# Two-layer recurrent block on one core: another order of ScalarE's work in layer 2

## The chip, the core and the metric

The kernel runs on one core of a Trainium2 chip. The metric is the device time of one execution in microseconds, the median of several executions.

## What is computed

The input x has 2 sequences of 1024 tokens with 256 features. Each of two layers computes `x = x + s * silu(f)`, where s is an attention of the normalised x, and f is a feed-forward part of the same normalised x. Layer 1 has attention over 1024 keys and a mixture of 64 experts. The change lies in layer 2, cut here to its core:

```python
xn = layernorm(x)
qkv = xn @ weight_qkv.T            # 16 heads of 16, 4 key/value heads
# the attention runs over the leading axis, which has length 2: token t of
# sequence 0 sees itself, token t of sequence 1 sees both
s = softmax(causal(q k / 4)) v @ weight_proj.T
h = gelu(bitlinear(xn, w_fc))      # 256 -> 1024 features
f = bitlinear(h, w_proj)           # 1024 -> 256 features
# bitlinear: layer norm of the input, then a product with ternary weights
x = x + s * silu(f)
```

## The kernel before

Layer 2 runs in eight pairs, p = 0 to 7. A pair is one tile of 128 tokens of sequence 0 with the same tile of sequence 1. Each engine has its own instruction stream, written out by hand, one loop over p each. An engine carries its stream out strictly in order, so a wait on a semaphore holds everything behind it. In this text, "round p" is the stretch from the scale `zhalf` of pair p to the scale `zhalf` of pair p+1.

What the engines do for a pair, with the function and the line in the profile:

- **TensorE** (lines 1507 to 1517): `turn_x` (1428) transposes the normalised tokens; `qkv` (1441); `fc` (1454) computes the 1024 hidden features in four groups j = 0 to 3 of eight matmuls, each group into one of three banks of PSUM, so that a group must wait until the gelu three groups before it has emptied its bank; `down1` (1487) multiplies the hidden features with the second weights in two halves, each as soon as its high and low part are there; `square_sums` (1494) ends this with the semaphore `z_ps`; `turn_att` (1464) and `project` (1472) finish the attention. Its order is `turn_x(p+1)`, `down1(p)`, `square_sums(p)`, `turn_att(p)`, `qkv(p+1)`, `project(p)`, `fc(p+1)`.
- **ScalarE** (lines 765 to 785): `gelu(p, j)` (704), four for a pair, out of PSUM; `high(p, h)` (720) rounds half h of the gelus to float16, and needs the gelus 2h and 2h+1; `square` (712) squares a half; `take_qkv` (693, 695); `gate2` (753) are two tanh of the product of `down1`, scaled by `zhalf`; `take_s1` (744) are the two copies of the attention's projection, scaled by the same `zhalf`; `half_tanh` (731) is the attention's weight.
- **VectorE** (lines 1167 to 1184): `low(p, h)` (1107) subtracts the high part from the hidden features, and needs `high(p, h)`; `moments` (1071 to 1079) of a later pair; `sum_squares` (1113, 1114, 1117); `low_x` (1096); `silu` (1064); `spreads` (1123 to 1126) and `newton` (1054 to 1059), a chain of small operations; `half_scale` (1134) writes `zhalf`; `normalise` (1086); `silu2` (1142); `score_difference` (1101). The order is `low(p, 1)`, `moments(p+2)`, `sum_squares(p)`, `low_x(p+1)`, `silu(p+3)`, `spreads(p)`, `newton`, `half_scale(p)`, `normalise(p+2)`, `silu2(p)`, `score_difference(p+1)`, `low(p+1, 0)`.
- **GpSimd** (lines 513 to 522): `attend(p)` (494, 496) needs `half_tanh(p)`; `total(p+4)` (465) for p up to 3, `add_gated(p+3)` (471, 472) for p up to 4 after `silu(p+3)`; `score_products(p+1)` (481 to 487); `finish(p)` (502, 503) needs `silu2(p)` and `take_s1(p)`.

The lines 502, 503, 494, 496, 465, 471 and 472 are tensor operations of GpSimd on data in SBUF.

Of the kernel before, what the change touches and what calls it, by code (L numbers as in the profile page):

```python
# [53 lines left out]
NP = NT // 2  # L54
# [21 lines left out]
def build(nc, q, router, Wkv, Wo, shared, sd, wgu_d, wdn_d, wqkv, wpo, wfc, wpj, out):  # L76
# [9 lines left out]
    with ExitStack() as ctx:  # L86
# [8 lines left out]
        def bk_(i):  # L95
            return two[i // 2][:, (i % 2) * 512:(i % 2) * 512 + 512]
# [193 lines left out]
        def z_bank(q):  # L290

            return bk_(5 + 2 * q)
# [232 lines left out]
        def _(sc):  # L525
# [149 lines left out]
            def gate(p):  # L675
                sc.wait_ge(acc_ready, p + 1)
                if p >= 2:
                    sc.wait_ge(x1_ready, p - 1)
                sc.activation(tg[p % 2], pair(xn, p), ACT.Tanh, scale=0.5).then_inc(gate_ready, 1)

            def high_x(p):
                sc.wait_ge(xT1_ps, p + 1)
                if p:
                    sc.wait_ge(fc_ps, 4 * p)
                sc.activation(xT_hi, bk_(0).rearrange("p (k n) -> p k n", k=KH), ACT.Copy).then_inc(xT_hi_ready, 1)

            def take_qkv(p):

                sc.wait_ge(scale_ready, p + 1)
                sc.wait_ge(qkv_ps, p + 1)  # L690
                if p >= 2:
                    sc.wait_ge(att_ready, p - 1)
                sc.activation(qkv1[p % 2], bk_(1)[:, 0:QKV1].rearrange("p (g c) -> p g c", g=NKV1), ACT.Copy,
                              scale=kvscale[p % 2][:, 1:2]).then_inc(qkv_ready, 1)
                sc.activation(kv0[p % 2], bk_(1)[:, QKV1:512].rearrange("p (g c) -> p g c", g=NKV1), ACT.Copy,
                              scale=kvscale[p % 2][:, 0:1]).then_inc(qkv_ready, 1)

            def gelu(p, j):

                n = 4 * p + j  # L700
                sc.wait_ge(fc_ps, n + 1)
                if p >= 2 and j % 2 == 0:
                    sc.wait_ge(lo_ready, 2 * (p - 2) + j // 2 + 1)
                sc.activation(hidT[p % 2][:, 512 * j:512 * j + 512], bk_(2 + n % 3), ACT.Gelu, scale=gwv[:, 0:1])\  # L704
                    .then_inc(gelu_ready, 1)

            def square(p, h):

                sc.wait_ge(gelu_ready, 4 * p + 2 * h + 2)
                if p:  # L710
                    sc.wait_ge(sqsum_ready, p)
                sc.activation(sq[:, HALF * h:HALF * h + HALF], hidT[p % 2][:, HALF * h:HALF * h + HALF], ACT.Square)\
                    .then_inc(sq_ready, 1)

            def high(p, h):

                sc.wait_ge(gelu_ready, 4 * p + 2 * h + 2)
                if p >= 2:
                    sc.wait_ge(z_ps, p - 1)
                sc.activation(hiT[p % 2][:, HALF * h:HALF * h + HALF], hidT[p % 2][:, HALF * h:HALF * h + HALF], ACT.Copy)\  # L720
                    .then_inc(hi_ready, 1)

            def own_value(p):

                if p:
                    sc.wait_ge(attT_ps, p)
                sc.activation(att_h[0], heads(kv0[p % 2][:, :, HD1:2 * HD1]), ACT.Copy).then_inc(att0_ready, 1)

            def half_tanh(p):
                sc.wait_ge(dif_ready, p + 1)  # L730
                sc.activation(td[:, :], dif[:, :], ACT.Tanh, scale=0.5 / HD1 ** 0.5).then_inc(td_ready, 1)

            def take_attT(p):
                sc.wait_ge(attT_ps, p + 1)
                sc.activation(attT, bk_(6).rearrange("p (s k n) -> p s k n", s=2, k=KH), ACT.Copy).then_inc(attT_ready, 1)

            def take_s1(p):

                sc.wait_ge(s1_ps, p + 1)
                if p >= 2:  # L740
                    sc.wait_ge(out_ready, p - 1)
                sc.wait_ge(zhalf_ready, p + 1)
                for q_ in range(GT):
                    ins = sc.activation(s1[p % 2][:, q_, :], bk_(6)[:, D * q_:D * q_ + D], ACT.Copy,
                                        scale=zhalf[p % 2][:, q_:q_ + 1])
                ins.then_inc(s1_ready, 1)

            def gate2(p):
                sc.wait_ge(zhalf_ready, p + 1)
                if p:  # L750
                    sc.wait_ge(zu_ready, GT * p)
                for q_ in range(GT):
                    sc.activation(tz[:, q_, :], z_bank(q_)[:, 0:D], ACT.Tanh, scale=zhalf[p % 2][:, q_:q_ + 1])\
                        .then_inc(ztanh_ready, 1)
# [10 lines left out]
            for p in range(NP):  # L765
                own_value(p)
                half_tanh(p)
                high(p, 1)
                for h_ in range(2):
                    square(p, h_)  # L770
                if p + 1 < NP:
                    high_x(p + 1)
                if p + 3 < NP:
                    gate(p + 3)
                take_attT(p)
                if p + 1 < NP:
                    take_qkv(p + 1)
                gate2(p)
                take_s1(p)
                if p + 1 < NP:  # L780
                    gelu(p + 1, 0)
                    gelu(p + 1, 1)
                    high(p + 1, 0)
                    gelu(p + 1, 2)
                    gelu(p + 1, 3)

# [776 lines left out]
```

## Time and profile before

| | us |
|---|---|
| median of three executions | 470.88 |
| lowest, highest | 468.42, 472.22 |
| profiled execution, its own time | 469.96 |
| its span from the first to the last instruction | 468.0 |
| granted TensorE clock, mean over the span | 0.937 of full speed |

Layer 2's pairs take from about 324 us to the end at 468 us. Over the whole span TensorE's matmuls are busy for 75%, VectorE 64%, GpSimd 57%, ScalarE 44%. These are shares over stages with different limits; what a change in a stage is worth is read from the chain of waits in that stage.

### The profile page before, as it was taken

The page shows a single profiled execution, that of the slowest core. Times are in us where ns is not written, and L with a number is a line of the kernel's source. Part 1 is how long each engine was busy: PE and PEld are TensorE (multiplying, and loading weights), DVE is VectorE, ACT ScalarE, POOL GpSimd, SP SyncE. Part 2 cuts the span into 40 slices and gives each one's busy share as a digit, 9 for nine tenths or more (in the row PEclk, how much of TensorE's full clock was granted, in tenths as well). Part 3 has the DMA queues.
Part 4 walks back from the last instruction along what each step waited for, and adds up shares of the span by engine and source line. Part 5 has one row for each costly group of instructions (what it writes and reads, how often), then busy time and mean ns, then how long its engine had stood idle before and what let it go on. Part 6 is the DMA issues. An engine that isn't in the chain of part 4 may idle for free.

```text
span 468.0 us, 6901 instructions
## 1 busy us (share of the span) xinstructions
PE 352.9 (75%) x2114; PEld 272.6 (58%) x2114; DVE 298.4 (64%) x864; ACT 204.5 (44%) x483; POOL 266.5 (57%) x272
## 2 busy tenths in 40 slices
PE   0999878687989687897998898106577767676774
PEld 0884345475877566686776777105366556565663
DVE  4929993555654253455666474246979778788766
ACT  1344242633443234643444453013563754745781
POOL 6440004177878667778888787472865566352550
PEclk9999997999999899998999999856999799799999
DMA  8760036968788798776877755490000000000000
GB/s 275 280 201 0 1 103 202 301 160 215 185 180 194 200 255 199 181 180 140 196 169 188 178 96 70 76 327 4 0 22 1 23 2 24 23 1 23 24 22 22
DMA packets 37558, 57.86 MB, mean 124 GB/s; under 512 B 6075, under 2 KB 27155, under 8 KB 37139
## 3 DMA queue, kind: packets, MB, share of 16 engines
q1 hardware_dynamic: 25235, 38.55, 25.5%
q0 software_dynamic: 12288, 18.88, 22.0%
q8 instruction: 17, 0.28, 0.3%
q14 instruction: 18, 0.15, 0.1%
HBM read 39.69 MB, written 17.73 MB: 123 GB/s over the span
## 4 chain that ended last, share of the span: by engine, by line
DVE 29%; PE 24%; DMA 13%; issue 12%; ACT 11%; POOL 10%; SPq 0%; ACTq 0%; POOLq 0%; DVEq 0%
DMA acc_d<-W,idxE 8%; POOL acc_d L457 5%; ACT W L704 3%; DMA W<-tok_d,idxE 3%; POOL W L437 3%; PE two L1320 3%; PE two L1368 3%; PE two L1284 3%; ACT A L720 2%; PE two L1193 2%; DVE F L1113 2%; DVE A L1107 2%; PE two L1380 2%; DVE ni L1054 1%; DMA x<-in_q 1%
## 5 line engine op out<-in xcount | busy, mean ns | idle before, releaser
L457 POOL DMA_INDIRECT acc_d<-W,idxE x64 | 102.4, 1599 | 30.7 <-issue 13.0
L437 POOL DMA_INDIRECT W<-tok_d,idxE x56 | 56.7, 1012 | 62.5 <-DMA tok_d<-F 45.7
L1019 DVE SCALAR_TENSOR_TENSOR W<-W,two 128x88 f32<-128x88 f32 x64 | 15.6, 244 | 63.8 <-ACT W L648 62.0
L632 ACT ACTIVATE W<-two 128x256 f32<-128x256 f32 x64 | 24.4, 381 | 51.7 <-PE two L1357 51.1
L1487 PE MATMUL two<-W,A 128*128 128x257 f16 x256 | 34.3, 294 | 16.6 <-DVE A L1107 16.6
L1487 PEld LDWEIGHTS two<-W,A 128*128 128x128 f16 x256 | 26.0, 105 | 25.0 <-issue 20.2
L1107 DVE TENSOR_TENSOR A<-W,A 128x1024 f16<-128x1024 f32 x16 | 26.7, 1670 | 21.4 <-ACT A L720 21.4
L1320 PE MATMUL two<-A,v 128*128 128x128 f32 x256 | 33.1, 284 | 6.7 <-issue 6.7
L1454 PE MATMUL two<-F,wfcT 128*128 128x256 f16 x256 | 31.0, 277 | 9.3 <-ACT W L704 9.3
L1320 PEld LDWEIGHTS two<-A,v 128*128 128x128 f32 x256 | 32.0, 199 | 8.9 <-issue 8.4
L1357 PE MATMUL two<-ident,W 128*128 128x128 f32 x112 | 22.8, 286 | 14.9 <-DMA W<-tok_d,idxE 12.7
L989 DVE TENSOR_SCALAR W<-two,W 128x256 f32<-128x256 f32 x56 | 26.8, 479 | 10.7 <-PE two L1380 6.7
L1454 PEld LDWEIGHTS two<-F,wfcT 128*128 128x128 f16 x256 | 25.0, 99 | 14.6 <-ACT W L704 10.7
L1368 PE MATMUL two<-W 128*128 128x176 f32 x160 | 31.9, 324 | 0.3 <-ACT W L639 0.2
L1357 PEld LDWEIGHTS two<-ident,W 128*128 128x128 f32 x112 | 14.2, 144 | 27.8 <-DMA W<-tok_d,idxE 17.2
L1284 PE MATMUL two<-kT,vT 128*128 128x512 f32 x64 | 30.1, 592 | 0.0
L886 DVE TENSOR_REDUCE nmax<-two 128x1 f32<-128x1024 f32 x16 | 19.6, 1223 | 14.9 <-PE two L1284 14.9
L1380 PE MATMUL two<-W 88*128 88x256 f32 x80 | 25.1, 396 | 1.1 <-DVE W L989 0.7
L1368 PEld LDWEIGHTS two<-W 128*128 128x128 f32 x160 | 25.1, 198 | 0.9 <-issue 0.9
L1428 PE MATMUL two<-ident,F 128*128 128x128 f32 x32 | 6.2, 329 | 22.9 <-DVE F L1086 22.9
L600 ACT ACTIVATE A<-two,nmax 128x1024 f32<-128x1024 f32 x16 | 17.8, 1113 | 10.0 <-DVE nmax L886 9.6
L471 POOL TENSOR_TENSOR F<-F,A 128x512 f32<-128x512 f32 x8 | 10.1, 1266 | 19.1 <-DVE F L1064 19.0
(217 smaller groups left out, 884.6 us busy)
## 6 DMA issues: line engine op xcount, KB each, us to landing
W<-in_gu SPq DMA_DIRECT2D x20, 352.0 KB
F<-in_gu SPq DMA_DIRECT2D x12, 352.0 KB
acc_d<-xn SPq DMA_DIRECT2D x8, 512.0 KB, 4.2
W<-in_dn SPq DMA_DIRECT2D x20, 176.0 KB
F<-in_dn SPq DMA_DIRECT2D x12, 176.0 KB
x<-in_q SPq DMA_DIRECT2D x4, 512.0 KB, 7.1
A<-in_Wo SPq DMA_DIRECT2D x1, 2048.0 KB, 13.0
tok_d<-xn SPq DMA_DIRECT2D x4, 512.0 KB, 4.3
```

Source lines behind the costliest of these rows:

```text
L437: pool.indirect_dma_start(out=xg[n % XR], out_offset=None, in_=tok_d[:, :], in_offset=bass.IndirectOffsetOnAxis(ap=idxE[:, n:n + 1], axis=0))\
L457: pool.indirect_dma_start(out=acc_d[n % 2][:, :], out_offset=bass.IndirectOffsetOnAxis(ap=idxE[:, n:n + 1], axis=0), in_=ysb[n % YS], in_o ...
L632: sc.activation(xgT[n % 2], bk_(2)[:, 0:D].rearrange("p (k n) -> p k n", k=KH), ACT.Copy)\
L989: ve.tensor_scalar(ysb[n % YS], bk_(3)[:, 0:D], xg[n % XR][:, D + n:D + n + 1], 0.5, ALU.mult, ALU.mult)\
L1107: ve.tensor_tensor(loT[p % 2][:, cols], hidT[p % 2][:, cols], hiT[p % 2][:, cols], ALU.subtract)\
L1284: ins = pe.matmul(two[2][:, 512 * h:512 * h + 512], vT[:, rows], kT[:, at:at + 512], start=True, stop=True)
L1320: ins = pe.matmul(bk_(1)[:, 0:P], v[:, (ORDER[t] // NP) * NP + i, :], probT[t % 2][:, i, :], start=(i == 0), stop=(i == 7))
L1357: ins = pe.transpose(bk_(2)[:, P * k:P * k + P], xg[n % XR][:, P * k:P * k + P], ident[:, :])
L1368: ins = pe.matmul(gu[n % 2], xgT[n % 2][:, k, :], wgu[r][:, n % WG, k, :], start=(k == 0), stop=(k == KH - 1))
L1380: pe.matmul(bk_(3)[:, 0:D], hT[n % 2], wdn[(n // WG) % WR][:, n % WG, :], start=True, stop=True)\
L1454: ins = pe.matmul(to, wfcT[:, k, P * c:P * c + P], part[:, k, :], start=(i == 0), stop=(i == 3))
L1487: pe.matmul(z_bank(q_)[:, 0:D + 1], part[p % 2][:, at:at + P], wpj2[:, c, 0:D + 1], start=(c == 0 and part is hiT), stop=(c == FF1 // P - ...
```

## The change

In ScalarE's loop over the pairs, `gelu(p+1, 0)` and `gelu(p+1, 1)` are put ahead of `gate2(p)`, and `high(p+1, 0)` is put between `gate2(p)` and `take_s1(p)`. Then follow `gelu(p+1, 2)` and `gelu(p+1, 3)` as before. The same instructions are issued, with the same waits, and no other engine's stream is changed. For p = 7 there is no next pair and the order stays.

```diff
@@ -775,12 +775,14 @@
                 take_attT(p)
                 if p + 1 < NP:
                     take_qkv(p + 1)
-                gate2(p)
-                take_s1(p)
                 if p + 1 < NP:
                     gelu(p + 1, 0)
                     gelu(p + 1, 1)
+                gate2(p)
+                if p + 1 < NP:
                     high(p + 1, 0)
+                take_s1(p)
+                if p + 1 < NP:
                     gelu(p + 1, 2)
                     gelu(p + 1, 3)
```

## Rows read from the trace of the kernel before

**Rows 1.** Waits, 343.7 to 468 us: us in total, times, longest us.

```profile
ACT F L753 <- DVE zhalf L1134: 18.6, 8, 3.5
```

**Rows 2.** Timeline of VectorE: start us, us, what. Five of eight `zhalf`.

```profile
343.69 0.29 DVE L1134 TENSOR_SCALAR zhalf<-ny,gwc 128x2 f32<-128x2 f32 x1
...
380.70 0.23 DVE L1134 TENSOR_SCALAR zhalf<-ny,gwc 128x2 f32<-128x2 f32 x1
...
399.18 0.23 DVE L1134 TENSOR_SCALAR zhalf<-ny,gwc 128x2 f32<-128x2 f32 x1
...
433.11 0.24 DVE L1134 TENSOR_SCALAR zhalf<-ny,gwc 128x2 f32<-128x2 f32 x1
...
447.71 0.29 DVE L1134 TENSOR_SCALAR zhalf<-ny,gwc 128x2 f32<-128x2 f32 x1
```

**Rows 3.** Chain that ended last, rounds 2 and 5: start us, us, what.

```profile
387.31 1.61 DVE A L1107
...
435.57 0.70 ACT W L704
```

**Rows 4.** Timeline of ScalarE, rounds 2 and 5; in brackets idle before, releaser.

```profile
380.96 0.84 ACT L753 ACTIVATE F<-two,zhalf 128x256 f32<-128x256 f32 x2 [3.46 <-DVE zhalf L1134]
381.69 0.84 ACT L744 ACTIVATE F<-two,zhalf 128x256 f32<-128x256 f32 x2
382.40 1.28 ACT L704 ACTIVATE W<-two,gwv 128x512 f32<-128x512 f32 x2
383.72 1.06 ACT L720 ACTIVATE A<-W 128x1024 f16<-128x1024 f32 x1
384.68 1.25 ACT L704 ACTIVATE W<-two,gwv 128x512 f32<-128x512 f32 x2
...
386.23 1.05 ACT L720 ACTIVATE A<-W 128x1024 f16<-128x1024 f32 x1
...
433.38 0.84 ACT L753 ACTIVATE F<-two,zhalf 128x256 f32<-128x256 f32 x2 [0.45 <-DVE zhalf L1134]
```

**Rows 5.** Timeline of TensorE: the matmuls of `fc` in rounds 0, 2 and 5.

```profile
342.85 2.78 PE L1454 MATMUL two<-F,wfcT 128*128 128x256 f16 x24
...
378.20 2.78 PE L1454 MATMUL two<-F,wfcT 128*128 128x256 f16 x24
...
433.62 3.66 PE L1454 MATMUL two<-F,wfcT 128*128 128x256 f16 x32
```

**Rows 6.** Timeline of GpSimd, round 2: `finish`, `attend`, `total`.

```profile
382.70 1.27 POOL L502 TENSOR_TENSOR F<-F 128x512 f32<-128x512 f32 x1 [2.46 <-ACT F L744]
...
386.42 0.62 POOL L494 TENSOR_TENSOR F<-F,td 128x256 f32<-128x256 f32 x1 [1.11 <-ACT td L731]
...
387.80 2.26 POOL L465 TENSOR_TENSOR xn<-xn,F 128x512 f32<-128x512 f32 x1
```

**Rows 7.** Timeline of VectorE, round 2: `moments`, first two sums of squares.

```profile
388.85 0.74 DVE L1071 BATCH_NORM_STATS2 st<-x 128x6 f32<-128x256 f32 x2
...
390.19 1.22 DVE L1113 TENSOR_TENSOR F<-W 128x1024 f32<-128x1024 f32 x1
391.44 0.69 DVE L1114 TENSOR_TENSOR F<-F 128x512 f32<-128x512 f32 x1
```

**Rows 8.** Timeline of VectorE ahead of `zhalf` of pair 0.

```profile
333.03 1.53 DVE L1113 TENSOR_TENSOR F<-W 128x1024 f32<-128x1024 f32 x1
334.60 1.10 DVE L1114 TENSOR_TENSOR F<-F 128x512 f32<-128x512 f32 x1
```

**Rows 9.** Timeline of GpSimd in the same stretch.

```profile
333.56 1.59 POOL L496 TENSOR_TENSOR F<-F 128x256 f32<-128x256 f32 x1
335.11 1.71 POOL L465 TENSOR_TENSOR xn<-xn,F 128x512 f32<-128x512 f32 x1
```

**Rows 10.** Busy time of TensorE and its granted clock (PEclk) in two stretches.

```profile
334.00:337.15 3.15, 0.00 (x1) 1.00 0.00 0
337.70:341.00 3.30, 3.30 (x17) 0.50 0.00 0
```

## The prediction

> **What bounds the kernel now.** I read the views in this order: the waits of layer 2, then VectorE's timeline for the length of a round, then the chain that ended last, then the timelines of the four engines beside each other. ScalarE stands at `gate2` for `zhalf` eight times, 18.6 us in all and up to 3.5 us at once [rows 1]: before that it has nothing to do, although work exists that could run. A round in the middle takes 399.18 - 380.70 = 18.48 us, the one from 433.11 to 447.71 takes 14.60 us [rows 2]. Rounds 0 to 3 have the long length and rounds 5 and 6 the short one; round 4 lies between. In round 2 the chain goes from `zhalf` through ScalarE (both tanh, both copies, all gelus, both high parts) to `low` at 387.31 on VectorE, which then works without a gap to the next `zhalf` [rows 2 to 4]. In round 5 the chain goes through TensorE's `fc` and the second gelu at 435.57 instead, and `zhalf` is there long before [rows 2, 3, 5]. So in rounds 1 to 4 what lies on ScalarE behind `zhalf` sets the pace; in rounds 5 and 6 it is what lies behind `fc`. The change moves work from the one place to the other.
>
> **Rounds 1 to 4: the gelus leave the chain.** In round 2 `fc` begins at 378.20 and its first three groups need 2.78 us, 0.93 us a group [rows 5]. In round 5, where nothing holds the second gelu but its group, it starts 435.57 - 433.62 = 1.95 us after the first matmul [rows 3, 5]. In round 2 that gives 378.20 + 1.95 = 380.15. The two gelus are spaced 1.28 - 0.70 = 0.58 us [rows 3, 4], so `gate2` could follow at 380.73, and `zhalf` releases it at 380.96 [rows 4]: both gelus are hidden in the 3.46 us of idle time, with 0.23 us to spare. From there the spacings of the same rows go on: 0.73 us for `gate2` (high part at 381.69), 0.96 us for the high part (384.68 - 383.72; copies at 382.65), 0.71 us for the copies (gelu 2 at 383.36), 1.55 us from gelu 2 to the second high part (386.23 - 384.68), which starts at 384.91 rather than 386.23. **Gain: 1.32 us in each of four rounds**, at this point of the chain. `fc`'s fourth group, which waited for the first gelu, comes some 2 us earlier as well; it was not late.
>
> What comes earlier on ScalarE meets GpSimd, though, and this takes some of it back. `finish` waits for the copies, which end at 383.46 now rather than at 382.53, 0.93 us later, while `half_tanh` and the low parts are earlier. The trace shows what happens when the two engines meet. Line 502 takes 1.27 us, and `total` has the same shape; in round 2 it starts at 387.80, lasts 2.26 us and so ends 1.14 us after `low`, which ran until 388.92 [rows 3, 6]. And ahead of pair 0's `zhalf` the two take turns: line 496 lasts 1.59 us (started just behind line 1113), line 1114 lasts 1.10 us rather than 0.69 us, `total` 1.71 us [rows 7 to 9]. One engine's operation is held until the other's ends, and a held one goes next. (The Trainium skill, page SBUF — State Buffer, section Who interferes with whom, says that a VectorE operation with two inputs in SBUF and a GpSimd operation that reads SBUF block each other for the whole instruction. By that rule the operations with one input in SBUF, as `moments`, are free; the trace agrees, since line 1071 takes 0.74 us for its two operations beside `total` and none of them is held [rows 7].)
>
> In the order after the change: the first `low` now runs from 382.8 to 384.0, ahead of `finish`, whose two operations of 1.27 us follow until about 386.55. The second `low` is ready at 386.03 and held to 386.55, ending at 387.65. That is as long (1.6 us) as before, when `attend` held it: no gain, no loss. Then come line 494 (0.62 us) and line 496 (the 0.7 us up to `total`'s start [rows 6]) until 389.0, in the time of `moments`, which `total` used before. Line 1113 (390.19 before [rows 7]) wants to start at 388.9, and is held by 0.1 us. `total` is next in the queue when line 1113 ends, and line 1114 is held for its length, 1.14 us. So where `total` exists (rounds 0, 1 and 2, as it is called for p up to 3 and the round behind `zhalf` of p has the `attend` of p+1) the gain is nearly gone. Rounds 1 and 2: -1.32 + 0.1 + 1.14 = **-0.1 us each**. Rounds 3 and 4 have no `total`: -1.32 + 0.1 = **-1.2 us each**. The bounds of this cost are 0 (GpSimd gets through in other gaps) and 1.5 us (the holds of both `low` and the two sums fully on top).
>
> **Round 0: neither.** Here `fc` begins at 342.85, only 0.84 us ahead of `zhalf` at 343.69, where in round 2 the lead is 2.50 us [rows 2, 5]. The second gelu starts at 342.85 + 1.95 = 344.80, and `gate2` behind it at 345.38, not at 344.01. It loses 1.37 us and wins back the same 1.32 us; the second high part stays where it is, within 0.1 us. But `finish` is now later by more than 2 us and the hold on the sums comes here too: 0.05 + 0.1 + 1.14 = **+1.25 us**.
>
> **Rounds 5 and 6: the change costs.** `gate2` started at 433.38 [rows 4], when `fc` had just begun (433.62). It and the copies filled the time until the second group was there at 435.57. Now they stand behind the second gelu: 0.73 + 0.73 us come on the chain, less 0.14 us because a tanh can follow a gelu 0.58 us after its start while the high part had to wait 0.72 us for its end. That is **+1.32 us** until the second high part, and here this chain ends in the squares and sums. The GpSimd side: the copies end 3.7 us later (438.68 rather than 433.38 + 0.73 + 0.84 = 434.95), `finish` ends at about 441.6, and `attend` (0.62 + 0.73 us), which used to be done beside `low`, now falls on lines 1113 and 1114. Line 494 holds the one by 0.2 us; line 496 costs the other about 0.4 us, as in rows 8 (1.10 - 0.69 us). Sum **+1.9 us each** (bounds 1.3 and 2.3).
>
> **Pair 7** has the same order as before: nothing.
>
> The sum: +1.25 - 0.1 - 0.1 - 1.2 - 1.2 + 1.9 + 1.9 = **+2.4 us**. Against the profiled execution's own 469.96 us that is 472.4 us. The median of the runs shown is 0.9 us above that execution, so 470.88 + 2.4 = 473.3 us. The bounds: with GpSimd's cost at nothing everywhere, 0.05 - 4 x 1.32 + 2 x 1.32 = -2.6 us; with all of its upper ends, about +4 us.
>
> **Rivals.**
> - *The holds by GpSimd don't add up* (gain of the reordering alone): -2.6 us, 468.3 us. For it: in round 2 the same two engines collide already and the cost there is hardly on the chain, and the order of few tenths of a microsecond decides. Against it: rows 8 and 9 show the very pattern. Chance 0.22.
> - *TensorE's clock falls at the wrong place* (slower). Ahead of pair 0's `zhalf` TensorE idles for 3.15 us and then works at 0.50 (1.2 GHz) from 337.70 to 341.00 [rows 10]; this is in `turn_att`, `qkv` and `project`, and it is why `fc`'s lead there is 1.66 us shorter. After the change the idle time of TensorE in a round is shifted: the gap inside `fc` goes, and the gap ahead of `square_sums` grows by some 1.2 us in rounds 1 and 2, since the second half of `down1` runs 1.3 us earlier while the sums come only 0.1 us earlier. If the clock falls there, the second gelu starts at 381.81, `gate2` behind it at 382.39 rather than at 380.96, and the round loses 1.43 us against my sum. It decides only in the new order: before, 2.50 us of lead covered it. Two or three such rounds give +5.3 to +6.7 us, 476.2 to 477.6 us. For it: round 0. Against it: rounds 1 and 3 of the kernel before have stretches at 0.50 too, but during `down1`, where they cost nothing. Chance 0.17. (The Trainium skill, page TensorE: Matmul & The Clock Gate, section What's actually happening, has the array at half rate after idleness and at full rate after sustained work. Before pair 0 the trace agrees.)
> - *It does nothing*: gains and losses cancel, or the second gelu is just too late to be covered in all rounds: 470.9 us, chance 0.11.
>
> My forecast has 0.5.
>
> **How the numbers follow.** No change can be told from a change below 1% (4.7 us) here. Faster by more than that needs 466.2 us, beyond even the first rival: 0.04. Slower by more than that needs 475.6 us: the clock rival nearly whole, and a little of the forecast's upper end: 0.19. The rest, 0.77, is within 1%. The range takes in most of the first rival and of the clock rival: 468.6 to 476.8 us.
>
> **What the profile after would show.** In round 2: two gelus ahead of `gate2`, no idle time between `fc`'s third and fourth group, `gate2` within 0.1 us of `zhalf`'s end, line 720's second start 4.0 us after `gate2` rather than 5.3 us. Round 3 near 17.3 us. Line 1114 near 1.8 us in rounds 0 to 2, and `total` near 2.3 us. Rounds 5 and 6 near 16.5 us, with ScalarE waiting for `fc` and no longer for `zhalf`. The prediction is wrong if `total` finds its place inside `moments` (rounds 1 and 2 then gain over a microsecond), if rounds 5 and 6 don't lengthen, or if a stretch of clock 0.50 lies on `qkv` or `project` in rounds 1 to 4.

## The result, and the profile after

The changed kernel takes 475.88 us (median of 20 executions, 470.32 to 478.72) against 471.35 us (20 executions of the kernel before). The ratio is **1.0073, 95% interval 1.0041 to 1.0105: +3.4 us**. It leaves out executions over 1.5% above the fastest of their kernel (of the changed one four, with the profiled one of 478.72 us), and so is less than the 4.5 us between the medians. The forecast was +2.4 us and "within 1%".

The profiled execution has a span of 476.7 us, 8.7 us more than before, and 4.2 us of these lie ahead of `zhalf` of pair 0, in work that the change doesn't touch. So the rounds are compared, not the spans. In its profile the lines of VectorE and TensorE are two higher: `zhalf` is line 1136, `low` 1109, the sums 1115, 1116 and 1119, `fc` 1456. The timeline of VectorE, `zhalf` of pairs 0, 2, 3, 5 and 6, answers to [rows 2]:

```profile
347.88 0.23 DVE L1136 TENSOR_SCALAR zhalf<-ny,gwc 128x2 f32<-128x2 f32 x1
...
387.15 0.23 DVE L1136 TENSOR_SCALAR zhalf<-ny,gwc 128x2 f32<-128x2 f32 x1
...
405.30 0.23 DVE L1136 TENSOR_SCALAR zhalf<-ny,gwc 128x2 f32<-128x2 f32 x1
...
438.32 0.24 DVE L1136 TENSOR_SCALAR zhalf<-ny,gwc 128x2 f32<-128x2 f32 x1
...
454.65 0.29 DVE L1136 TENSOR_SCALAR zhalf<-ny,gwc 128x2 f32<-128x2 f32 x1
```

All eight of them, in both profiles, give the length of each round in us:

| round | before | after | measured | forecast |
|---|---|---|---|---|
| 0 | 18.54 | 19.70 | +1.16 | +1.25 |
| 1 | 18.47 | 19.57 | +1.10 | -0.1 |
| 2 | 18.48 | 18.15 | -0.33 | -0.1 |
| 3 | 18.47 | 18.77 | +0.30 | -1.2 |
| 4 | 15.46 | 14.25 | -1.21 | -1.2 |
| 5 | 14.60 | 16.33 | +1.73 | +1.9 |
| 6 | 14.65 | 16.36 | +1.71 | +1.9 |
| all | 118.67 | 123.13 | +4.46 | +2.4 |

Rounds 0, 2, 4, 5 and 6 came as forecast. Rounds 1 and 3 are 1.2 and 1.5 us above it. ScalarE's timeline shows round 2 as it was meant, and then round 5 (it answers to [rows 4]):

```profile
385.73 0.69 ACT L704 ACTIVATE W<-two,gwv 128x512 f32<-128x512 f32 x1 [1.77 <-PE two L1456]
386.60 0.69 ACT L704 ACTIVATE W<-two,gwv 128x512 f32<-128x512 f32 x1 [0.19 <-PE two L1456]
387.42 0.84 ACT L753 ACTIVATE F<-two,zhalf 128x256 f32<-128x256 f32 x2
388.14 1.05 ACT L720 ACTIVATE A<-W 128x1024 f16<-128x1024 f32 x1
389.09 0.84 ACT L744 ACTIVATE F<-two,zhalf 128x256 f32<-128x256 f32 x2
...
391.35 1.09 ACT L720 ACTIVATE A<-W 128x1024 f16<-128x1024 f32 x1
...
439.91 0.69 ACT L704 ACTIVATE W<-two,gwv 128x512 f32<-128x512 f32 x1 [1.77 <-PE two L1456]
440.78 0.69 ACT L704 ACTIVATE W<-two,gwv 128x512 f32<-128x512 f32 x1 [0.19 <-PE two L1456]
441.37 0.83 ACT L753 ACTIVATE F<-two,zhalf 128x256 f32<-128x256 f32 x2
```

In round 2 both gelus run in the time in which ScalarE stood idle, and the tanh starts 0.27 us after `zhalf` begins (0.26 us before). The second high part starts 3.93 us after the tanh rather than 5.27 us: 1.34 us won. In round 5 `zhalf` begins at 438.32, and the tanh, which could follow it, stands behind the second gelu until 441.37.

What takes the gain back in round 2 is seen on GpSimd and VectorE. Their two timelines, cut to this place (they answer to [rows 6, 7]):

```profile
394.57 0.73 POOL L496 TENSOR_TENSOR F<-F 128x256 f32<-128x256 f32 x1
395.25 1.27 POOL L465 TENSOR_TENSOR xn<-xn,F 128x512 f32<-128x512 f32 x1
```

```profile
395.43 2.17 DVE L1115 TENSOR_TENSOR F<-W 128x1024 f32<-128x1024 f32 x1
397.64 0.69 DVE L1116 TENSOR_TENSOR F<-F 128x512 f32<-128x512 f32 x1
...
449.57 1.10 DVE L1116 TENSOR_TENSOR F<-F 128x512 f32<-128x512 f32 x1
```

`total` (line 465) starts 0.18 us ahead of the first sum, and this lasts 2.17 us instead of 1.22 us. In round 5 it is `attend` that holds the second sum, 1.10 us instead of 0.69 us.

The rest of the loss is TensorE's clock. The busy time of TensorE with its granted clock (the number behind the busy time and its count) in four stretches: the first two lie ahead of `zhalf` of pair 1, the third ahead of that of pair 2, the last ahead of that of pair 3:

```profile
358.30:360.90 2.60, 0.00 (x0) 1.00 0.00 0
362.10:366.00 3.90, 3.90 (x17) 0.56 0.00 0
381.70:384.60 2.90, 2.90 (x21) 1.00 0.02 6
...
399.90:403.40 3.50, 3.50 (x16) 0.53 0.02 5
```

From 362 to 366 us and from 400 to 403 us `qkv` and `project` run mostly at half clock (1.2 GHz); from 381.7 to 384.6 they run at full clock (2.4 GHz). The first gelu ahead of the gate of pair 1 starts at 367.75, after `zhalf` at 367.58, where for pair 2 it is 1.4 us ahead of it. So rounds 1 and 3, which begin with these two, are the long ones. The first stretch is the idle time ahead of the sums' product. Such long rounds are no oddity of this execution: the experiments below have one in a profile of 469.26 us and one in a profile of 470.74 us.

### The profile page after: what moved, and what is told of

Same layout as the page of the kernel before. It is cut to its first block, busy times and chain, and to the rows that moved or that the text cites. A ratio compares the mean times of both kernels' runs of the same rounds, so it can differ in the third digit from the quotient of the medians.

```text
span 476.7 us, 6901 instructions
## 1 busy us (share of the span) xinstructions
PE 357.1 (75%) x2114; PEld 276.9 (58%) x2114; DVE 298.9 (63%) x864; ACT 204.9 (43%) x483; POOL 274.1 (58%) x272
## 4 chain that ended last, share of the span: by engine, by line
PE 36%; DVE 22%; DMA 12%; ACT 11%; issue 10%; POOL 8%; SPq 0%; ACTq 0%; POOLq 0%; DVEq 0%
DMA acc_d<-W,idxE 6%; DMA W<-tok_d,idxE 4%; PE two L1286 4%; PE two L1370 3%; ACT A L720 3%; POOL acc_d L457 3%; PE two L1230 3%; DVE F L1115 3%; PE two L1322 3%; PE two L1443 3%; PE two L1195 3%; PE two L1382 2%; POOL W L437 2%; PE two L1456 2%; PE two L1474 2%
## 5 line engine op out<-in xcount | busy, mean ns | idle before, releaser
L457 POOL DMA_INDIRECT acc_d<-W,idxE x64 | 102.8, 1606 | 33.0 <-issue 14.7
L1489 PE MATMUL two<-W,A 128*128 128x257 f16 x256 | 32.1, 280 | 24.6 <-DVE A L1109 24.6
L1489 PEld LDWEIGHTS two<-W,A 128*128 128x128 f16 x256 | 24.4, 99 | 31.9 <-issue 28.6
L1109 DVE TENSOR_TENSOR A<-W,A 128x1024 f16<-128x1024 f32 x16 | 23.0, 1438 | 16.6 <-ACT A L720 16.6
L1286 PE MATMUL two<-kT,vT 128*128 128x512 f32 x64 | 32.1, 625 | 0.0
L888 DVE TENSOR_REDUCE nmax<-two 128x1 f32<-128x1024 f32 x16 | 19.6, 1224 | 18.4 <-PE two L1286 18.4
L1456 PE MATMUL two<-F,wfcT 128*128 128x256 f16 x256 | 29.6, 275 | 0.0
L704 ACT ACTIVATE W<-two,gwv 128x512 f32<-128x512 f32 x32 | 21.2, 697 | 16.1 <-PE two L1456 16.1
L502 POOL TENSOR_TENSOR F<-F 128x512 f32<-128x512 f32 x7 | 10.4, 1488 | 26.2 <-ACT F L744 26.2
```

Of the source, the lines that this page charges most:

```text
L457: pool.indirect_dma_start(out=acc_d[n % 2][:, :], out_offset=bass.IndirectOffsetOnAxis(ap=idxE[:, n:n + 1], axis=0), in_=ysb[n % YS], in_o ...
L1109: ve.tensor_tensor(loT[p % 2][:, cols], hidT[p % 2][:, cols], hiT[p % 2][:, cols], ALU.subtract)\
L1286: ins = pe.matmul(two[2][:, 512 * h:512 * h + 512], vT[:, rows], kT[:, at:at + 512], start=True, stop=True)
L1456: ins = pe.matmul(to, wfcT[:, k, P * c:P * c + P], part[:, k, :], start=(i == 0), stop=(i == 3))
L1489: pe.matmul(z_bank(q_)[:, 0:D + 1], part[p % 2][:, at:at + P], wpj2[:, c, 0:D + 1], start=(c == 0 and part is hiT), stop=(c == FF1 // P - ...
```

## The experiments

Each ratio is against the kernel before, timed beside it; an interval reaches 0.3 to 0.6% (1.3 to 2.8 us) to either side. The diffs are shortened: they show the order of the calls, and leave out conditions that stay and, at `...`, other lines. All but two are against the changed kernel; the high part alone and the control of `total` are against the kernel before. "Rounds" are the lengths from the profile of that kernel, in us, before: 18.5, 18.5, 18.5, 18.5, 15.5, 14.6, 14.7.

**The new order in rounds 5 and 6 alone**, that of before in the others. The condition `ahead` stands in both places of the change; where it is false, the two gelus and the high part follow the copies.

```diff
-                if p + 1 < NP:
+                ahead = 5 <= p < LAST
+                if ahead:
```

> The new order only in rounds 5 and 6, where fc begins after zhalf; rounds 0 to 4 keep the order of before. My theory (in these rounds gate, copies and high part line up behind the second gelu): rounds 5 and 6 about 16.3 us instead of 14.6 us, +3.5 us in all, ratio 1.007, and rounds 0 to 4 unchanged. Rival (the loss of the changed kernel comes from TensorE's clock and from GpSimd in the rounds before): no change, ratio 1.000.

Measured: ratio 1.0062 (1.0030 to 1.0093), +2.9 us. Rounds 18.5, 18.5, 18.4, 18.5, 15.5, **16.33, 16.36**. The last two are those of the changed kernel, and the others those of before: the loss at the end of the layer is the order's own, and it is most of the result.

This profile also shows what a half clock on `qkv` and `project` costs in the old order, ahead of `zhalf` of pair 3 at 401.35 (TensorE's busy time and clock, then ScalarE):

```profile
395.60:399.00 3.40, 3.40 (x18) 0.52 0.02 5
```

```profile
401.61 0.84 ACT L753 ACTIVATE F<-two,zhalf 128x256 f32<-128x256 f32 x2 [2.01 <-DVE zhalf L1141]
```

The tanh still waits for `zhalf` and starts 0.26 us behind it, and round 3 has its 18.48 us. So in the old order this costs nothing; in the new one it costs 1.4 us (below).

**The new order in rounds 1 to 4 alone.**

```diff
-                if p + 1 < NP:
+                ahead = 1 <= p <= 4
+                if ahead:
```

> The new order only in rounds 1 to 4. My theory: rounds 1 and 2 18.1 us, rounds 3 and 4 17.3 and 14.2 us, so -3.1 us where TensorE's clock is full during qkv and project; each round whose gate finds the clock at 0.50 there is 1.4 us longer. With one or two such rounds -1.7 to -0.3 us, ratio 0.996 to 0.999. Rival (the clock does not matter): -3.1 us, ratio 0.993. Rival (what the middle rounds gain is always taken back): 1.000 or more.

Measured: 0.9934 (0.9902 to 0.9965), -3.1 us. Rounds 18.50, **18.23, 18.12, 18.80, 14.26**, 14.60, 14.65. Together with the run before this takes the change apart: what it gains in the middle it gives back at the end. Round 0 is in neither run; with its +1.2 us the parts make +1.0 us by the ratios, against +3.4 us, and the 2.4 us between are within the intervals of the three ratios taken together. In the profiles the parts are +3.3, -1.5 and +1.2 us against +4.5 us: the changed kernel's has one more round at half clock (1.4 us). Round 3 was the long one here too, with TensorE's clock at 0.50 from 394.2 to 397.6 us, ahead of `zhalf` of pair 3. By the ratio my rival that the clock does not matter came closer (0.993), though the interval takes in both; the profile has one such round, and the median of the timed executions is 1 us below the profiled one, so this run alone doesn't decide between them.

**The gelus ahead, the copies ahead of the high part.**

```diff
                 gate2(p)
-                high(p + 1, 0)
                 take_s1(p)
+                high(p + 1, 0)
```

> Two gelus ahead of the gate in all rounds, but the copies again ahead of the high part, so that finish is released 1 us earlier. The second high part starts at the same time as in the changed kernel. If only ScalarE's order counts, the time is that of the changed kernel, +3.4 us against before. If GpSimd's collisions with the sums cost what the trace shows (0.94 us each in rounds 0 to 2), finish comes earlier and total fits beside moments again: rounds 0 to 2 about 0.9 us shorter each, +0.6 us against before.

Measured: 0.9995 (0.9968 to 1.0022), 3.6 us better than the changed kernel's ratio. But not for the reason that I gave. Rounds 19.33, 19.44, 17.92, 16.97, 13.94, 16.41, 16.45. The first sum is held as before (2.18 us), since `total` is still late. What is gone is the hold of the second `low` (VectorE's timeline, round 2):

```profile
385.01 1.53 DVE L1108 TENSOR_TENSOR A<-W,A 128x1024 f16<-128x1024 f32 x1 [0.68 <-ACT A L720]
387.52 1.23 DVE L1108 TENSOR_TENSOR A<-W,A 128x1024 f16<-128x1024 f32 x1 [0.98 <-ACT A L720]
```

`finish` now collides with the first `low`, which has time, and the second lasts 1.23 us rather than 1.54 us. That is 0.1 to 0.3 us a round in rounds 1, 2 and 4 against the changed kernel. This profile also has one round of half clock less than that of the changed kernel (1.4 us). The rounds of the two profiles differ by 2.7 us; what is left of the 3.6 us isn't explained.

**The high part alone ahead of the copies**, the gelus behind the gate as before.

```diff
                 gate2(p)
-                take_s1(p)
                 gelu(p + 1, 0); gelu(p + 1, 1); high(p + 1, 0)
+                take_s1(p)
```

> Only the third part of the change: the gelus stay behind the gate, but the first high part goes ahead of the copies. On ScalarE alone nothing changes for the second high part, so if only ScalarE's order counts: ratio 1.000. If GpSimd's collisions count: finish is released 2.3 us later and total falls on line 1113 in rounds 0 to 2, 0.9 to 1.1 us each, and up to 0.4 us in the others: +3 to +4 us, ratio 1.006 to 1.009.

Measured: **1.0213 (1.0153 to 1.0273), +10 us**, far more than I expected. Rounds 19.53, 18.90, 20.73, 20.22, 15.62, 15.74, 15.79. Round 1, whose gate finds the clock full, is 0.43 us longer than before, rounds 5 and 6 are 1.1 us longer: there the copies (0.72 us) are on the chain, plus 0.4 us of hold. I had expected 0.9 to 1.1 us in the first and at most 0.4 us in the last two, so the places are wrong, if not the sum. In rounds 2 and 3 TensorE's clock is at half for 6.8 us, over the whole of `qkv` and `project` (busy time and clock of TensorE):

```profile
377.50:384.30 6.80, 6.80 (x26) 0.50 0.01 2
398.00:404.80 6.80, 6.64 (x26) 0.50 0.01 2
```

and `fc` begins at 384.79, 1.45 us behind `zhalf` (383.34), where it led by 2.50 us in [rows 2, 5]. ScalarE waits for `fc` behind the gate, and the high part and the copies follow only then. The rounds of this profile give +7.9 us, and 0.7 us more lie ahead of round 0; the last 1.4 us aren't assigned.

**The hold of the sums taken away by moving `total`.** First to before the attention of pair 0:

```diff
+            for i in range(3, NP):
+                total(i)
             score_products(0)
             add_gated(2)
-            total(3)
             for p in range(NP):
                 attend(p)
-                if p + 4 < NP:
-                    total(p + 4)
```

> The changed kernel, with the totals of pairs 4 to 7 done early by GpSimd, in its idle time before the attention of pair 0, so that none falls on the sums. If the hold of line 1113 by total is a cost on the chain: rounds 0 to 2 0.9 us shorter each, so 2.8 us faster than the changed kernel, +0.6 us against before, and the sums take 1.23, 0.69, 0.42 us. If it is hidden: the time of the changed kernel, +3.4 us.

Measured: 1.0033 (1.0000 to 1.0067). Rounds **17.28, 17.27, 17.36, 17.27, 14.25**, 16.33, 16.37: without a hold by `total`, and with the clock at full speed throughout, rounds 0 to 3 are 1.2 us shorter than before each, which is the whole gain of the order. But `zhalf` of pair 0 comes 41.1 us after pair 0's gate (ScalarE's first tanh of the layer) rather than 37.0 us. GpSimd's and VectorE's timelines show why:

```profile
315.31 6.13 POOL L465 TENSOR_TENSOR xn<-xn,F 128x512 f32<-128x512 f32 x5
```

```profile
314.26 1.10 DVE L1063 TENSOR_TENSOR nt<-ny 128x4 f32<-128x4 f32 x1
315.40 1.19 DVE L1064 SCALAR_TENSOR_TENSOR nt<-nt,nv 128x4 f32<-128x4 f32 x1
316.62 1.18 DVE L1065 SCALAR_TENSOR_TENSOR ny<-nt,ny 128x4 f32<-128x4 f32 x1
...
321.49 0.16 DVE L1063 TENSOR_TENSOR nt<-ny 128x4 f32<-128x4 f32 x1
```

The roots of pair 0 are operations of 4 elements in a row, 0.16 us each. Six of them wait for one whole operation of GpSimd each, five for a `total`: 1.1 to 1.2 us. An engine's idle time was not free, because the other engine's chain ran beside it.

**`total` behind `zhalf`**, in three kernels: with the new order for p up to 4, with the order of before (the control), and with the changed kernel's order in all rounds.

```diff
                 attend(p)
-                if p + 4 < NP:
-                    total(p + 4)
 ...
+                if p + 4 < NP:
+                    pool.wait_ge(zhalf_ready, p + 1)
+                    total(p + 4)
                 if p < LAST:
                     finish(p)
```

> The new order only for p up to 4, and total(p+4) of GpSimd moved from behind attend(p) to behind zhalf of pair p, where GpSimd idles, so that it meets neither the sums nor the chain ahead of zhalf. If hold and clock are what ate the gain: rounds 0 to 3 17.3 us, round 4 14.3 us, rounds 5 and 6 14.6 us as before, so -6 us in all, ratio 0.987. If the place of total doesn't matter, it is the run with the order in rounds 1 to 4 over again, ratio 0.993. If total now holds normalise and with it the first low part to the chain's cost, 0.995 or more.

> The kernel before with total(p+4) moved behind zhalf of pair p and ScalarE's order untouched: the control. My theory: total ran in the time of moments there and cost nothing, so moving it changes little: rounds 18.4 to 18.5 us, ratio 0.998 to 1.000 (line 1117 of pair 0 is freed of its hold of 1.1 us, but that is before round 0). Rival (total is a cost in either order): 2 us faster, 0.996.

> The changed kernel in all rounds, with total(p+4) behind zhalf of pair p. My theory: rounds 0 to 3 17.3 us where the clock is full, round 4 14.3 us, rounds 5 and 6 16.3 us as in the changed kernel: -2.5 us against before, ratio 0.994 to 0.995. The distance to the run with the new order for p up to 4 alone is then what rounds 5 and 6 cost, 3.4 us. Rival (the place of total doesn't matter): ratio 1.007.

| kernel | ratio | 95% | rounds |
|---|---|---|---|
| new order for p up to 4 | 0.9915 | 0.9879 to 0.9951 | 17.89, 17.89, 17.94, 17.88, 14.24, 14.61, 14.64 |
| order of before | 0.9976 | 0.9942 to 1.0009 | 18.38, 18.41, 18.38, 18.37, 15.46, 14.59, 14.66 |
| order as changed | 0.9973 | 0.9936 to 1.0010 | 17.89, 17.88, 17.95, 17.57, 14.25, 16.32, 16.38 |

The control says that `total` was no cost in the old order (0.1 us a round). With the new order the rounds are shorter than before, but 17.9 us and not 17.3: the third expectation of the first came in part. `total` is followed by `finish`, which now takes its turn ahead of the first `low` (both timelines, round 1 of the first kernel):

```profile
363.76 1.26 POOL L502 TENSOR_TENSOR F<-F 128x512 f32<-128x512 f32 x1 [1.26 <-ACT F L745]
365.10 2.13 POOL L503 TENSOR_TENSOR x<-x,F 128x512 f32<-128x512 f32 x1
```

```profile
360.98 1.68 DVE L1094 TENSOR_SCALAR F<-x,mv,ny 128x256 f32<-128x256 f32 x2
...
363.84 4.48 DVE L1115 TENSOR_TENSOR A<-W,A 128x1024 f16<-128x1024 f32 x2
```

The two `low` together last 4.48 us; unheld, one takes 1.23 us. `normalise` (line 1094) is held first, so `low` is late and `finish` is ahead of it. The difference between the first and the third kernel is in rounds 5 and 6, 3.4 us there, as expected; the ratios differ by 0.6% (2.7 us).

**All totals early, but behind pair 0's transposes**, new order for p up to 4.

```diff
+            pool.wait_ge(xT_hi_ready, 1)
+            for i in range(3, NP):
+                total(i)
             score_products(0)
 ...
```

> The new order for p up to 4 and all totals of GpSimd in its idle time before pair 0's attention, but only once pair 0's transposes have been taken, so that they no longer hold the roots of pair 0. If the early totals of the run before cost its 4 us only by holding these roots: zhalf of pair 0 no later than before, rounds 0 to 3 17.3 us, round 4 14.3 us, rounds 5 and 6 14.6 us, -6 us in all, ratio 0.987. If pair 1's roots or the products of pair 0 are held to the chain's cost instead: 0.990 to 0.994. If totals anywhere before the rounds cost what they save: 0.995 or more.

Measured: 0.9911 (0.9878 to 0.9945). Rounds 18.04, 17.29, 17.27, 17.29, 14.24, 14.62, 14.64, -5.3 us in all; `zhalf` of pair 0 comes 38.1 us after its gate (37.0 before), so -4.2 us, which is the ratio. The roots of pair 1 are held now, as the second of my cases had it; its `normalise` takes 2.78 us.

**The best version: totals 3 and 4 early, 5 to 7 behind `zhalf`.**

```diff
+            pool.wait_ge(xT_hi_ready, 1)
+            total(3)
+            total(4)
 ...
+                if p + 5 < NP:
+                    pool.wait_ge(zhalf_ready, p + 1)
+                    total(p + 5)
```

> The new order for p up to 4; the totals of pairs 3 and 4 early but only two of them, so that they end as pair 1's roots begin, those of pairs 5, 6 and 7 behind zhalf of pairs 0, 1 and 2. If both losses seen so far are what I take them for (1.1 us before round 0 from held roots of pair 1; 0.6 us in each round whose total lies behind zhalf): from the gate of pair 0 to zhalf of pair 0 at most 37.0 us, rounds 0 to 2 17.9 us, round 3 17.3 us, round 4 14.3 us, rounds 5 and 6 14.6 us: -4.5 to -5.5 us, ratio 0.988 to 0.990. If two early totals hold pair 1's roots as well: 0.991 or more, no better than the two versions before.

Measured: **0.9883 (0.9841 to 0.9924), -5.5 us**, the lowest ratio of all. `zhalf` of pair 0 comes 36.7 us after the gate; rounds 17.90, 17.88, 17.88, 17.27, 15.67, 14.59, 14.66. Round 4 is the one with half clock on its `qkv` (408.4 to 411.8 us); without that it would be 14.3 us as in the others. These rounds and the start give -3.2 us; the profiled execution is 1.7 us longer than the median of its kernel, and the rest isn't assigned. Its interval overlaps those of the two versions before it, so it is the best by its middle value only.

**Filling TensorE's idle time ahead of the sums.** Ten matmuls in each round whose product nobody reads.

```diff
             def square_sums(p):
+                for _ in range(10):
+                    pe.matmul(z_bank(0)[:, 260:512], ones16[:, :], wpjT[:, 0, 0:252],
+                              start=True, stop=True)
                 pe.wait_ge(sqsum_ready, p + 1)
```

> The changed kernel with ten matmuls of 252 columns in each round ahead of the wait for the square sums, whose result nobody reads; they fill 1.1 us of TensorE's idle time there and end before the wait does. If the low clock on qkv and project is what makes rounds 1 and 3 of the changed kernel long (19.6 and 18.8 us): no stretch at 0.50 there, rounds 1 and 2 18.1 us, round 3 17.3 us, round 0 17.3 to 19.7 us, so 2.5 to 3 us faster than the changed kernel, ratio 1.001 against before. If the clock does not matter or falls anyway: as the changed kernel, 1.007. If the fillers delay the sums' product: slower than 1.007.

Measured: 1.0071 (1.0029 to 1.0114), just the changed kernel. Rounds 19.70, 18.28, 19.59, 17.27, 14.24, 16.33, 16.37. The fillers take 1.24 us and leave 1.69 us of idle time; still the clock falls, in other rounds (busy time and clock):

```profile
336.80:340.20 3.40, 3.40 (x14) 0.51 0.00 0
374.30:377.70 3.40, 3.40 (x15) 0.50 0.00 0
```

So what the low clock costs is shown (below), but not that the gap ahead of the sums is what brings it on; this remedy fails.

## Why the prediction was right, step by step

**Gelus off the chain, 1.32 us a round.** Right: 1.34 us in round 2 up to the second high part, and rounds 0 to 3 are 1.1 to 1.3 us shorter where nothing else interferes (totals early: 17.27 to 17.36 us).

**GpSimd takes it back in rounds 0 to 2.** Right in the rounds, one operation off, and too high by 0.2 us in rounds 1 and 2. I had the second sum (line 1114) held for 1.14 us and the first (line 1113) for 0.1 us, and the second `low` as long as before. Measured: it is the first sum that `total` holds, 2.17 - 1.22 = 0.95 us, since `total` came first by 0.18 us; the second takes its 0.69 us, and `total` its 1.27 us rather than the 2.3 us that I expected. The second `low` takes 1.54 us. Moving `total` away shows the 0.9 us: 18.15 us against 17.27 us. Rounds 2 and 4: -0.33 and -1.21 us against -0.1 and -1.2.

**Round 0.** Right: +1.16 against +1.25 us (the terms as I wrote them add up to 1.29). Its second high part starts 5.59 us after `zhalf` in both kernels, so the order gains nothing there. With totals early no half clock lies on `qkv` or `project` of pair 1 ahead of `zhalf` of pair 0, and round 0 is 17.28 us like the others. So here the clock was in my sum.

**Rounds 5 and 6.** Right, +1.72 us each against +1.9, and shown alone by the first experiment (+2.9 us by the ratio, 3.4 us in the rounds). In round 5 the second high part starts 445.29 - 438.32 = 6.97 us after `zhalf` rather than 5.69 us, +1.28 us against my +1.32; `attend` costs the second sum 0.41 us, and the 0.2 us that I had for the first did not come (1.23 us).

**What failed: the clock stood beside the sum and not in it.** I had it as a rival with 0.17, in "two or three such rounds" of 1.43 us. In the profiled execution two rounds have it, 1 and 3. The prediction named this as a sign that it is wrong, and the sign came: from 400 to 403 us, in round 2, the clock is at half on `qkv` and `project`. Leaving this term out of the sum for rounds 1 to 4 is the step that failed; what it was measured at is 1.42 us in each of two rounds. Its price was right: round 1 against round 2 of the same profile, 19.57 - 18.15 = 1.42 us; in the kernel with fillers 19.59 - 18.28 = 1.31 us. Without them the rounds of the profile would give +1.6 us; the measured mean of +3.4 us would be met by 1.3 such rounds in an average execution (worked out, not counted; with the 4.5 us between the medians of all executions it would be two). My +2.4 us was near because the holds and the last rounds were put too high, by 0.8 us over all rounds, while the clock was missing. So the size came out in part by luck, two errors of opposite signs; the sign and five of seven rounds came out by their own working.

**The rivals.** That the holds don't add up is refuted: 18.15 us with `total` on the sums, 17.27 us without. That it does nothing is refuted in every round. Faster by over 1% was out of reach for this order: it took the old order in rounds 5 and 6 and another place for `total` to get to -5.5 us.

**What stays open:** why the clock falls in some rounds and not in others. A gap of 2.76 us stands ahead of the product of the sums of pairs 1, 2 and 3 in the changed kernel, and the clock falls behind the first and the third. With fillers the gap was 1.69 us and it fell as well; in the first experiment it fell behind one of 1.66 us in the old order.

## What to carry to other kernels

An order of work that is right for one steady state can be wrong for another of the same loop: look which of two releases comes last in each round, and switch the order where that switches. Before moving anything on one engine, write down which engine its later results release, and what the other side of a shared resource is doing at that new time; an idle engine isn't a free place if its operations hold a chain of small ones. And where a slack of 2.5 us is used up to 0.2 us, all that varied below it before, such as a clock, is on the chain from then on: the same half clock cost nothing in the old order and 1.4 us in the new.

## What the runs showed of the hardware that was not expected

- One GpSimd operation of 128x512 float32 (1.2 us) holds a VectorE operation of 128x4 (0.16 us) for its whole length, and back to back the two take turns: six small operations took 1.1 to 1.2 us each beside six of GpSimd's.
- Whoever starts first has the turn: `total` 0.18 us ahead of a sum cost 0.95 us, where before it had run beside `moments`, and moving it away gave 0.1 us a round.
- The granted clock of TensorE stays at 0.50 for 3.4 us or 6.8 us. It fell in some rounds and not in others of the same order. Where it covers `down1` it costs nothing. On `qkv` and `project` it costs nothing in the old order (round 3 of the first experiment, 18.48 us) and 1.3 to 1.4 us in the new one.
